# Attention plus butterfly layer on one core: the first unit's row maxima in two parts, and eighteen unread matmuls in the head

## The reference

```
q, k, v = x @ w_q, x @ w_k, x @ w_v                  # 16 heads of 64
p = softmax(q k^T / sqrt(64) + causal mask)          # over 1024 keys
x = layernorm(x + (p v) @ w_o)
h = butterfly_up(x @ W_exp + b_exp)                  # 9 stages over 512
h = gelu(h + up_bias)
y = butterfly_down(h) @ W_con + b_con + down_bias
out = layernorm(x + y)                               # eps 1e-5
```

## Time and profile before

| | |
|---|---|
| median of 3 runs | 1036.18 us (1035.88 to 1036.36) |
| the profiled execution's own time | 1035.9 us |
| its span | 1034.2 us |
| PE busy | 1007.0 us, 97% of the span |
| DVE / POOL / ACT busy | 75% / 73% / 59% |
| PE idle in 29 to 33 us and 33 to 46 us of the span | 3.3 us and 3.2 us |
| mean granted TensorE clock | 0.993 |

### The profile page before, as it was taken

How to read it: one execution, slowest core, us unless ns; L and a number is a source line. 1 busy time by engine, 2 the same in 40 slices (tenths; PEclk the granted TensorE clock), 3 DMA queues, 4 the chain that set the end, 5 groups by cost and what they waited for, 6 DMA issues and landing times.

```text
span 1034.2 us, 17742 instructions
## 1 busy us (share of the span) xinstructions
PE 1007.0 (97%) x5816; PEld 697.7 (67%) x5816; DVE 778.0 (75%) x2112; ACT 613.1 (59%) x1246; POOL 750.9 (73%) x715
## 2 busy tenths in 40 slices
PE   6799999999999999999999999999999999999997
PEld 4566676676666776676666766767666766765687
DVE  7767777877777777878788778877778888785356
ACT  3555656566656656666556656666555656665544
POOL 6567887777768887777778877777778887777510
PEclk8899999999999999999999999999999999999999
DMA  6233122233222222232232222332222222320002
GB/s 190 62 83 82 45 72 53 62 83 83 58 68 62 63 65 60 63 83 63 70 76 58 62 56 55 83 83 63 66 60 74 63 57 57 83 64 22 22 11 73
DMA packets 48602, 68.71 MB, mean 66 GB/s; under 512 B 15191, under 2 KB 25083, under 8 KB 48510
## 3 DMA queue, kind: packets, MB, share of 16 engines
q1 hardware_dynamic: 48510, 67.57, 25.3%
HBM read 31.11 MB, written 2.36 MB: 32 GB/s over the span
## 4 chain that ended last, share of the span: by engine, by line
PE 92%; DVE 3%; DMA 2%; ACT 1%; issue 1%; POOL 0%; SPq 0%; POOLq 0%; ACTq 0%
PE O L717 25%; PE WORK L631 14%; PE SC L692 14%; PE SC L696 13%; PE WORK L644 6%; PE WORK L679 3%; PE WORK L607 3%; PE WORK L609 3%; PE WORK L608 3%; PE WORK L772 2%; PE WORK L617 1%; PE WORK L619 1%; PE WORK L618 1%; DVE WORK L991 1%; DMA R<-RROW 1%
## 5 line engine op out<-in xcount | busy, mean ns | idle before, releaser
L863 ACT ACTIVATE PR<-SC 128x512 f32<-128x512 f32 (+3 forms) x768 | 352.3, 490 | 263.9 <-PE SC L696 231.4
L519 POOL TENSOR_TENSOR SUM<-SUM,PR 128x1024 f32<-128x1024 f32 (+3 forms) x256 | 419.0, 1637 | 14.8 <-POOL SUM L528 0.5
L991 DVE CUSTOM_DVE_ANT_0 WORK<-WORK,CMASK 128x128 f32<-128x128 f32 (+3 forms) x512 | 239.3, 514 | 65.7 <-PE WORK L631 65.6
L692 PE MATMUL SC<-QH,KHL 128*128 128x512 f32 (+3 forms) x768 | 268.8, 356 | 3.1 <-ACT PR L863 3.0
L696 PE MATMUL SC<-QL,KH 128*128 128x512 f32 (+3 forms) x768 | 261.7, 346 | 3.3 <-DMA QL<-NROW 3.3
L504 POOL TENSOR_SCALAR_AFFINE_SELECT PR<-PR 128x256 f32<-128x256 f32 x256 | 105.9, 415 | 198.0 <-ACT PR L863 197.9
L631 PE MATMUL WORK<-KHL,QH 128*128 128x512 f32 (+3 forms) x768 | 226.5, 365 | 5.9 <-DMA KH<-KHL 4.1
L717 PE MATMUL O<-PR,VLO 128*64 128x512 f32 (+3 forms) x1024 | 200.0, 522 | 0.3 <-DVE OT L1075 0.3
L692 PEld LDWEIGHTS SC<-QH,KHL 128*128 128x128 f32 x768 | 145.2, 189 | 60.7 <-ACT PR L863 28.5
L631 PEld LDWEIGHTS WORK<-KHL,QH 128*128 128x128 f32 x768 | 136.7, 191 | 59.3 <-issue 35.4
L994 DVE TENSOR_REDUCE MP<-WORK 128x1 f32<-128x512 f32 x256 | 164.1, 684 | 4.8
(11 more groups left out here) (132 smaller groups left out, 1099.0 us busy)
## 6 DMA issues: line engine op xcount, KB each, us to landing
QH<-QH SPq DMA_DIRECT2D x128, 128.0 KB, 2.4
KH<-KHL SPq DMA_DIRECT2D x128, 128.0 KB, 2.3
R<-RROW SPq DMA_DIRECT2D x64, 256.0 KB, 3.8
SW<-in_L_ffn_up_weights_dram SPq DMA_DIRECT2D x9, 512.0 KB, 4.4
SW<-_L_ffn_down_weights_dram SPq DMA_DIRECT2D x9, 512.0 KB, 4.3
out_dram<-X SPq DMA_DIRECT2D x7, 256.0 KB, 2.3
X<-in_L_attn_x_BSE_dram SPq DMA_DIRECT2D x3, 512.0 KB, 4.5
X<-in_L_attn_x_BSE_dram SPq DMA_DIRECT2D x2, 256.0 KB, 3.3
```

The source lines that it names most:

```text
L519: nc.gpsimd.tensor_tensor(total, total, prob(unit, s), ALU.add).then_inc(add_done, 1)
L692: nc.tensor.matmul(dst, KHL[:, par, h, kt * P:(kt + 1) * P], QH[:, par, h, q0:q0 + n], start=True, stop=False)
L863: nc.scalar.activation(prob(unit, s)[:, h, :], SC[use % NSC][:, 0:n], ACT.Exp, scale=K ** -0.5).then_inc(exp_done, 1)
L991: op = nc.vector.tensor_tensor_reduce(cols, cols, CMASK[:, CH - n:], 1.0, LOWEST, ALU.add, ALU.max, cell)
```

## The change

Three things are changed, all of them for unit 0 and the head:

1. PREFETCH has a new order: q and k of chunk 0, the first values, q of chunk 1, only the six max fillers of chunk 0, then k of chunk 1, the second values, and the q projection of unit 1. The fifteen max fillers of chunk 1 become fillers ("first", i) in unit 0's own steps 0 to 3 (FIRST_MAXES).
2. The rows of unit 0 are transferred in two parts, `first_rows(0)` and `first_rows(1)`, each with two DMAs of 2 KB, one for each head; DVE makes NROW once more in exchange. The first L724 (the former L696) of unit 0 waits for part 0, and that of step 4 for part 1.
3. `keep_warm` issues matmuls of 512 columns into SC[0], whose result nobody reads: six behind filler 3, one behind each of the six max fillers, and six behind filler 12, which makes eighteen.

```
+WARM_AFTER = {3: 6} | {n: 1 for n in range(4, 10)} | {12: 6}
...
+FIRST_MAXES = [(s, place, ("first", i)) for i, (s, place) in enumerate(
+    [(0, BETWEEN)] * 3 + [(0, BEHIND)] * 3 + [(1, BETWEEN)] * 4 + [(2, BETWEEN)] * 3 + [(3, BETWEEN)] * 2, CHUNK0_MAXES)]
...
-PREFETCH = [("proj", 0, 0), ("v", 0), ("proj", 1, 0), ("proj", 0, 1), ("v", 1), ("proj", 1, 1)] + MAXES + [("proj", 0, 0)]
+PREFETCH = [("proj", 0, 0), ("proj", 1, 0), ("v", 0), ("proj", 0, 1)] + MAXES[:CHUNK0_MAXES]
+PREFETCH += [("proj", 1, 1), ("v", 1), ("proj", 0, 0)]
...
+            def first_rows(c):
+
+                sp.wait_ge(nrow_made, c + 1)
+                for h in range(2):
+                    dst = QL[K:K + 1, 0, h, c * CH:(c + 1) * CH].rearrange("a (t c) -> a t c", t=TPC)
+                    row = h * TILES + c * TPC
+                    sp.dma_start(dst.bitcast(F32), NROW[row:row + TPC, :].bitcast(F32)).then_inc(m_landed, 16)
...
-            rows(0)
+            first_rows(0)
             for u in range(UNITS):
                 if u + 1 < UNITS:
                     copies(u + 1)
+                if u == 0:
+                    first_rows(1)
...
-                    if s == 0 and h == 0:
-                        pe.wait_ge(m_landed, (unit + 1) * 16)
+                    if (unit, s, h) == (0, 0, 0):
+                        pe.wait_ge(m_landed, 32)
+                    elif (s, h) == (0, 0) or (unit, s, h) == (0, FIRST_OF[1], 0):
+                        pe.wait_ge(m_landed, rows_landed(unit))
...
+            def keep_warm(times):
+
+                for _ in range(times):
+                    nc.tensor.matmul(SC[0][:, :], XTH[:, 0:P], XTH[:, 0:CH], start=True, stop=True)
...
             for n, f in enumerate(PREFETCH):
...
                 filler(-2 if n == 0 else -1, f, n)
+                keep_warm(WARM_AFTER.get(n, 0))
...
-                    if f == MAXES[-1]:
+                    if f == MAXES[-1] or (u < 0 and f == MAXES[CHUNK0_MAXES - 1]) or f == ("first", len(MAXES) - 1):
+                        made = 0 if u < 0 else 1 if f[0] == "first" else u + 2
```

More of the change, by code:

```diff
@@ L128 @@
 W1_SPLIT_AT = (UNITS - 1, 8)
+FIRST_MAXES = [(s, place, ("first", i)) for i, (s, place) in enumerate(
+    [(0, BETWEEN)] * 3 + [(0, BEHIND)] * 3 + [(1, BETWEEN)] * 4 + [(2, BETWEEN)] * 3 + [(3, BETWEEN)] * 2, CHUNK0_MAXES)]
+assert FIRST_MAXES[-1][2][1] == len(MAXES) - 1
 def unit_fillers(u):
     b, n = u // PAIRS, u % PAIRS
-    rows = []
+    rows = list(FIRST_MAXES) if u == 0 else []
     for s, place, f in FILLERS:
@@ L353, in prob, with rows_landed @@
             return PR[:, (unit * NS + s) % PRING, :, 0:n]
+        def rows_landed(unit):
+            return 64 + 16 * unit
         block = ctx.enter_context(nc.Block())
@@ L401, in copies @@
                             .then_inc(dup_landed[c], 16)
+            def first_rows(c):
[4 more added lines that the diff above has]
+                    sp.dma_start(dst.bitcast(F32), NROW[row:row + TPC, :].bitcast(F32)).then_inc(m_landed, 16)
             def rows(unit):
                 par = unit % 2
-                sp.wait_ge(nrow_made, (unit + 1))
+                sp.wait_ge(nrow_made, unit + 2)
                 dst = QL[K:K + 1, par, :, :].rearrange("a h (t c) -> a (h t) c", t=TILES)
@@ L446, in _ @@
             inverses(UNITS - 1)
-            sp.wait_ge(m_landed, 16 * UNITS)
+            sp.wait_ge(m_landed, rows_landed(UNITS - 1))
             for c in range(CHUNKS):
@@ L619, in filler @@
                         t = nc.tensor.matmul(out, XTL[:, lo:lo + P], WSV[:, 0, :], start=False, stop=True)
-                elif f[0] == "max":
-                    pieces = f[1]
-                    unit, nxt = u + 1, (u + 1) % 2
+                elif f[0] in ("max", "first"):
+                    pieces = f[1] if f[0] == "max" else MAXES[f[1]][1]
+                    unit = u + (f[0] == "max")
+                    nxt = unit % 2
+                    if f == ("first", CHUNK0_MAXES):
+                        evacuated(NUMBER[-1, ("proj", 0, 1)])
+                        evacuated(NUMBER[-1, ("proj", 1, 1)])
+                        pe.wait_ge(dup_landed[1], 64)
                     for c in range(CHUNKS):
@@ L823, in evacuate @@
                 w, free = WORK[at % NWORK], work_free[at % NWORK]
-                if f[0] in ("max", "out", "w2", "wo", "con", "bias"):
+                if f[0] in ("max", "first", "out", "w2", "wo", "con", "bias"):
                     return
@@ L999, in consume @@
                                                 negate=True).then_inc(negm_made, 1)
-                        dve.wait_ge(negm_made, u + 2)
-                        if u >= 0:
-                            dve.wait_ge(m_landed, (u + 1) * 16)
+                        dve.wait_ge(negm_made, made + 1)
+                        if made == 1:
+                            dve.wait_ge(m_landed, 32)
+                        elif made > 1:
+                            dve.wait_ge(m_landed, rows_landed(u))
                         for b in range(0, P, BLK):
```

## The result

The changed kernel is slower: 1045.68 us (median of 6 runs, 1044.01 to 1049.24) against 1035.99 us, ratio 1.0101 with a 95% interval of 1.0081 to 1.0120. Forecast was slower, at 1041.2 us with a range up to 1043.4: the right sign, but 9.7 us instead of 5.3 (on the medians; 8.9 us between the profiled spans). The six runs of the changed kernel spread over 5.2 us, the six of before over 0.9 (13 and 35 further runs of before, made beside the experiments, over 2.2 to 3.2).

A forecast was written before the change was run, and what follows sets the result against it. PE, busy 97% of the span, was taken as the bound, with only time before unit 0's step 5 counting. First wait -4.4, second wait and longer list +8.5, clock +1.2: +5.3, so 1041.2 us, range 1036.4 to 1043.4.

The forecast's parts named there:

- The frame: Whole kernel: from step 5 of unit 0 on PE gives no delay back, so only step 5's start counts.
- Head up to the row DMAs: Head: part 0's rows ready at about 20.1 us, KH pair at 19.3, row DMAs issued at 24.3 and 24.9.
- Landing: First row wait: rows queue behind SP's loads and land at 28.5 us, ending the wait 4.4 us earlier.
- The step that failed: First row wait's end: after some 4 us of unbroken work PE is at 2.4 GHz by 28.5 us.
- the three idle pieces of 0.6 us: DVE's list before step 4: idle 0.6 us at the start, before unit 1's k and before its chunk 1 q.
- the stretch from one L724 to the other: Unit 0, 28.5 to 48.55 us: DVE's list of 17.6 us, then two DMAs of 2.45 us.
- a fall of the clock once, at step 4: Step 4's wait: PE idles some 3.4 us, its clock falls to 1.2 GHz, costing 1.2 us.
- Step 4 to step 5: Unit 0, from step 4's L724 to step 5: PE needs 1.76 us, plus 1.2 us for the low clock.
- A hidden second part (1): Rival 1, unit 0: step 4 never waits for rows, so the kernel is faster, 1033.8 us; chance 0.10.
- rows that don't queue (2): Rival 2: rows don't queue behind loads (-1.7), step 4's clock stays high (-1.2), or both: 1039.5, 1040.0, 1038.3 us; chance 0.25.
- rival 3: Head: unread matmuls don't hold the clock, k of chunk 1 comes 2.6 us later; 1043.8 us; chance 0.07.
- Rival 4: No change: rows at 26.8, DVE idle pieces gone (-1.8), no clock loss; 1036.5 us; chance 0.16.

The follow-up runs named there:

- b: The kernel before with the same eighteen unread matmuls and nothing else of the change; 1035.37 us, ratio to before 0.9997.
- c: The changed kernel with first_rows(0) put ahead of SP's seven loads; 1040.51 us, ratio to before 1.0049.
- d: The changed kernel with 42 further unread matmuls in unit 0 to hold the clock, 18 of them in the first wait; 1042.39 us, ratio to before 1.0061.
- h: The changed kernel with first_rows(0) ahead of the loads and unread matmuls holding the clock in unit 0, none in the first wait; 1037.61 us, ratio to before 1.0017.
- j: As h, but with four of the fifteen chunk 1 fillers back in the head and one held place moved; 1036.99 us, ratio to before 1.0021.
- e: The kernel before with only the new order: k of each chunk ahead of the values; 1034.67 us, ratio to before 0.9990.
- f: The kernel before with twelve unread matmuls behind the last filler of the head; 1034.34 us, ratio to before 0.9986.
- g: The kernel before with both the new order of k and values and twelve unread matmuls at the head's end; 1034.53 us, ratio to before 0.9987.
- a: The changed kernel without its eighteen unread matmuls; 1046.38 us, ratio to before 1.0101.
- i: The changed kernel with only SP's last two loads (W_exp and X, 768 KB) moved behind first_rows(0); 1041.15 us, ratio to before 1.0050.

## Why the prediction was right in its sign and wrong in its size

- **The frame held.** Only what happens ahead of step 5 counts: the span behind it is 987.7 us against 988.0, 987.3 to 988.1 in b, c, d, h and j, and 988.6 to 989.0 in e, f and g. It is 989.7 in a, where the clock is 0.62 on the mean from 56 to 60 us, behind step 5, and 989.4 in i. So up to 2 us can move behind step 5, and not in the changed kernel.
- **Head up to the row DMAs: right.** NROW at 20.3 (forecast 20.1), KH pair at 19.88 (19.3), row DMAs at 24.86 (24.3); PE's pause before L724 is released by QL<-NROW at both places, as forecast.
- **Landing: right in kind, 1.2 us short.** 28.5 forecast (the terms give 28.6), 29.72 measured; 0.6 of it is the later issue. Experiments c and i show that the loads delay the rows, by taking them away from in front.
- **The step that failed: "By 28.5 PE has had some 4 us of unbroken work, and I take it to be at the high clock", and with it the three idle pieces of 0.6 us in DVE's list.** PE's last work before the wait was 2.5 us (22.4 to 24.9) at the high clock, and then came 4.8 us without any: it met the list at 1.2 GHz, and behind the pauses within it (1.8, 0.5 and 0.9 us, waiting for DVE) the clock fell again. DVE's work up to NROW was 15.6 us, as forecast (15.8). Its idleness was 4.7 us instead of 1.8: 1.15 at the start, 1.44 before k, 1.30 before q, 0.42 that I did not have, and the rest in gaps under 0.2. With the clock held (d) the three pieces were 0.59, 0.69 and 0.61, and the list took 17.4 us against the 17.6 forecast. So the stretch from one L724 to the other, put at 20.05 us, took 22.67, and 19.8 in d: the 20.05 was the value for the high clock. I had priced a fall of the clock once, at step 4, and not in the stretch ahead of it, though PE was idle for a quarter of that stretch already before (busy for 9.85 of 13.00 us).
- **Step 4 to step 5: right.** 3.05 us against 2.96, with a clock of 0.50 in 52 to 55; at the high clock it is 1.74 (d, h).
- **The sum.** Forecast 5.3, plus 1.2 (landing), 2.6 (clock in the list) and 0.1 (step 4 to 5), is the 9.2 measured at step 5 (55.44 - 46.23). The spans say 8.9, the runs' medians 9.7: the profiled run, at 1044.85 us, lies in the lower part of six that differ by up to 5 us.
- **The rivals.** A hidden second part (1) did not come; rows that don't queue (2) are refuted by i; the unread matmuls did hold the clock in the head, against rival 3, yet without them the time was the same. Rival 4 had the terms come out short; they came out long. Rival 1's 1033.8 was taken from the median of 1036.2, and the other times from the profiled run's 1035.9; it changes no verdict.

## What to carry to other kernels

Work that is moved off a bounding engine's critical stretch into a half-empty one needs room there for its whole length and for the wait that is put behind it: here 9.5 us of DVE work went into 4.8 us of idleness, and even the repaired split lost 1.8 us. A small transfer that is awaited belongs ahead of bulk loads that nobody awaits: here it paid for their bytes (2.0 us or more) and not only for their issues (0.8). And where a change makes TensorE pause repeatedly, ask for the clock of the whole stretch, and not for one fall: here the pauses kept its mean at 0.73 and cost 2.6 to 2.9 us.

## What the hardware showed that I had not expected

- The same DVE and ACT work with the same dependences took 19.9, 20.1 and 22.7 us at mean granted clocks of 1.00, 0.90 and 0.73, although DVE was busier than PE in the latter two (17.8 against 12.8 us, and 17.4 against 16.3). So a lower clock of TensorE lengthened a chain whose busiest engine was another, by 2.9 us between the changed kernel and d, which differ only in unread matmuls.
- Whether these pauses also make a kernel vary more from run to run is not shown. The changed kernel spread over 5.2 us in 6 runs, a over 3.6 and c over 3.9 in 4, and d, with the clock held, over 1.3 in 4; but b, whose profiled clock was high, spread over 4.1 in 10, and 35 runs of before over 3.2.
- Twelve unread matmuls of 512 columns took 2.91 us in d at the high clock and 4.52 in j, most of it at the low one, and 18 took 4.93 in d while the clock rose. A number of them that fits a wait at the high clock outlasts it at the low one, and then holds back what it stands ahead of.
